# Attention's q and k product from high and low halves, bf16 parts stored once, weights loaded after the rounds

## The reference

```python
x = L0_attn_x                                       # [16, 256, 128] float32
h = _layernorm(x, axis=-1) * (1 + ca) + sa
x = x + ga * _L0_attn_ref(h, L0_attn_w_qkv, ...)
...
qkv = x @ w_qkv + b_qkv                             # inside _L0_attn_ref: 16 heads of depth 8
q = _rope(q)
k = _rope(k)
scores = jnp.einsum('bhtd,bhsd->bhts', q, k) / jnp.sqrt(jnp.float32(D))
attn = jax.nn.softmax(scores, axis=-1)
out = jnp.einsum('bhts,bhsd->bhtd', attn, v)
...
return out @ w_fc + b_fc
```

## Time and profile before

| | us |
|---|---|
| median of 3 runs | 1827.18 (1826.78 to 1829.08) |
| the profiled execution | 1828.58 |
| its span | 1826.5 |
| TensorE busy | 1659.0, 91% |
| VectorE busy | 1366.2, 75% |
| ScalarE busy | 819.6, 45% |
| GpSimd busy | 691.8, 38% |

### The profile page before, as it was taken

How to read it: one execution, slowest core, us unless ns; L and a number is a source line. 1 busy time by engine, 2 the same in 40 slices (tenths; PEclk the granted TensorE clock), 3 DMA queues, 4 the chain that set the end, 5 groups by cost and what they waited for, 6 DMA issues and landing times.

```text
span 1826.5 us, 25499 instructions
## 1 busy us (share of the span) xinstructions
PE 1659.0 (91%) x7212; PEld 1027.0 (56%) x7212; DVE 1366.2 (75%) x2636; ACT 819.6 (45%) x1533; POOL 691.8 (38%) x628
## 2 busy tenths in 40 slices
PE   3888888869989999999999999999998899899999
PEld 2455555446655656556665565655655555555555
DVE  4777777656979988979969889799698587544444
ACT  1566767657644234243352342533525543433333
POOL 2011111100002945928739469187394475000000
PEclk9989989989999999999999999999999999999999
DMA  6554445246575877677767666666671111111110
GB/s 199 152 157 129 119 111 152 89 125 215 180 207 188 222 205 204 210 209 214 215 189 203 187 188 197 189 197 204 190 194 52 41 47 52 35 57 53 52 52 23
DMA packets 172698, 269.49 MB, mean 148 GB/s; under 512 B 23748, under 2 KB 61981, under 8 KB 170053
## 3 DMA queue, kind: packets, MB, share of 16 engines
q1 hardware_dynamic: 168691, 266.33, 49.9%
q10 hardware_dynamic: 1874, 1.36, 0.2%
q0 software_dynamic: 2048, 0.79, 0.2%
HBM read 233.78 MB, written 34.62 MB: 147 GB/s over the span
## 4 chain that ended last, share of the span: by engine, by line
PE 36%; DVE 16%; issue 10%; POOL 10%; ACT 3%; DMA 3%; SPq 1%; DVEq 0%; POOLq 0%; ACTq 0%
PE psum L1528 10%; PE psum L1368 6%; POOL e_prod L1986 6%; PE psum L1370 6%; PE psum L1369 6%; PE psum L1383 5%; DVE psum L1897 4%; POOL e_phi L1986 3%; DVE e_hm L1900 2%; DVE e_vbar L1755 2%; DVE e_y L1755 1%; DVE e_state L1850 1%; DMA e_ring<-w_split 1%; PE psum L1462 1%; DMA rw<-rw_fm 1%
## 5 line engine op out<-in xcount | busy, mean ns | idle before, releaser
L1694 ACT ACTIVATE e_gu<-psum 128x512 f32<-128x512 f32 (+1 forms) x368 | 219.3, 598 | 545.5 <-PE psum L1370 284.3
L1368 PE MATMUL psum<-e_hhi,e_ring 128*128 128x512 f32 x704 | 434.0, 616 | 19.7 <-DMA e_ring<-w_split 11.5
L1383 PE MATMUL psum<-e_hm,w_d 128*128 128x512 f32 (+1 forms) x736 | 382.6, 601 | 15.0 <-DVE e_hm L1903 7.2
L1986 POOL TENSOR_TENSOR e_prod<-e_state,e_phi 128x512 f32<-128x512 f32 x256 | 353.4, 1417 | 2.4 <-POOL e_phi L1986 1.7
L1897 DVE TENSOR_TENSOR psum<-psum,rw 128x512 f32<-128x512 f32 x352 | 243.4, 692 | 90.9 <-PE psum L1370 85.1
L1935 DVE TENSOR_TENSOR e_hm<-psum,rw 128x512 f32<-128x512 f32 x256 | 174.6, 688 | 178.0 <-ACT psum L1722 176.9
L1369 PE MATMUL psum<-e_hhi,e_ring 128*128 128x512 f32 x704 | 279.0, 396 | 0.0
L1370 PE MATMUL psum<-e_hlo,e_ring 128*128 128x512 f32 x704 | 278.8, 396 | 0.0
L1900 DVE TENSOR_TENSOR e_hm<-psum,e_gu 128x512 f32<-128x512 f32 x352 | 243.5, 692 | 39.4 <-ACT e_gu L1694 15.7
L1528 PE MATMUL psum<-e_hm,w_gu 128*128 128x512 f32 x512 | 262.9, 598 | 6.6 <-DVE w_d L1916 5.5
L1722 ACT ACTIVATE psum<-psum 128x512 f32<-128x512 f32 x256 | 148.8, 582 | 254.7 <-PE psum L1370 238.8
(11 more groups left out here) (304 smaller groups left out, 2181.0 us busy)
## 6 DMA issues: line engine op xcount, KB each, us to landing
e_ring<-w_split SPq DMA_DIRECT2D x308, 256.0 KB, 4.2
rw<-rw_fm SPq DMA_DIRECT2D x192, 176.0 KB
qk_parts<-at_part SPq DMA_DIRECT2D x96, 192.0 KB, 3.1
rw<-gates_fm SPq DMA_DIRECT2D x72, 256.0 KB, 3.2
w_split<-e_ring SPq DMA_DIRECT2D x44, 256.0 KB, 2.7
rw<-rw_fm SPq DMA_DIRECT2D x64, 160.0 KB
at_qs<-qk_parts SPq DMA_DIRECT2D x16, 576.0 KB
at_ks<-qk_parts SPq DMA_DIRECT2D x16, 576.0 KB
```

What stands on the lines that cost most here:

```text
L1368: pe.matmul(out, w_hi, x_hi, start=first, stop=False)
L1383: mm = pe.matmul(ps[:, ACC, :], weights_at(T, WD + P * j, P)[0:rows(j), :], hm[0:rows(j), slot(j), :], start=(j == 0), stop=(j == HT - 1))
L1694: a(act_g[0:r, j % 2, :], ps[0:r, GB[j % 2], :], ACT.Silu).then_inc(silu_done, 1)
L1986: ins = tt(out[:, at], x[:, at], y[:, at], op)
```

## The change

The q and k product is made from halves: `w_qk` and each `hb` are rounded to fp32r (`w_hi`, `hb_hi`, ScalarE), the rest after the subtraction is the low half (`w_lo` on VectorE, once; `hb_lo` on GpSimd, each round), and three products, high by high, low by high and high by low, are summed in PSUM. There is one buffer each for `hb_hi` and `hb_lo`. The parts are stored once (two transfers of 192 KB), and each stack is loaded by three transfers of 24 rows; those of `ks` read 8 rows three times. The 16 weight pieces are issued by SP after its last round, when all maxima are in. Buffers of the first gates' work now lie in `rest` and `rest2`. GpSimd's wait for `x_fm` stands in round 2 instead of ahead of the rounds.

```diff
-STACK_DMAS = 2
-OUT_DMAS = 2 * PARTS
+STACK_DMAS = 2 * PARTS
+OUT_DMAS = 2
...
-        bounce = nc.dram_tensor("qk_parts", [BUFS, 2, PARTS, PARTS, DEPTH, HEADS, SEQ], BF16, kind="Internal").ap()
+        bounce = nc.dram_tensor("qk_parts", [BUFS, 2, PARTS, DEPTH, HEADS, SEQ], BF16, kind="Internal").ap()
...
                 if f["proj"]:
-                    pe.wait_ge(h_ready, n + 3)
+                    pe.wait_ge(h_low, n + 3)
...
                     for c in range(2):
-                        mm = pe.matmul(ps[:, M0, c * SEQ:(c + 1) * SEQ], w_qk[:, c * P:(c + 1) * P], hb[:, (k + 2) % BUFS, :],
-                                       start=True, stop=True)
+                        out, at = ps[:, M0, c * SEQ:(c + 1) * SEQ], slice(c * P, (c + 1) * P)
+                        pe.matmul(out, w_hi[:, at], hb_hi[:], start=True, stop=False)
+                        pe.matmul(out, w_lo[:, at], hb_hi[:], start=False, stop=False)
+                        mm = pe.matmul(out, w_hi[:, at], hb_lo[:], start=False, stop=True)
                     mm.then_inc(qk_proj, 1)
...
+            dve.wait_ge(w_high, 1)
+            nc.vector.tensor_tensor(w_lo[:], w_qk[:], w_hi[:].bitcast(F32), ALU.subtract).then_inc(w_cut, 1)
             run(dve, iteration)
...
+                        act.wait_ge(h_ready, n + 4)
+                        if k > FIRST:
+                            act.wait_ge(qk_proj, n + 3)
+                        nc.scalar.activation(hb_hi[:], hb[:, (k + 3) % BUFS, :], ACT.Copy).then_inc(h_high, 1)
...
+            nc.scalar.activation(w_hi[:], w_qk[:], ACT.Copy).then_inc(w_high, 1)
             run(act, iteration)
...
                 if f["p1"]:
                     move_rows(n, k, 0)
+                if f["xn"]:
+                    pool.wait_ge(h_high, n + 4)
+                    nc.gpsimd.tensor_tensor(hb_lo[:], hb[:, (k + 3) % BUFS, :], hb_hi[:].bitcast(F32), ALU.subtract).then_inc(h_low, 1)
                 if f["tail"]:
                     b = n - 2
+                    if k == 2:
+                        pool.wait_ge(T["x_fm_in"], 16)
...
-            pool.wait_ge(T["x_fm_in"], 16)
             run(pool, iteration)
...
             def load_stack(buf, stack, q):
 
-                sp.dma_start(stack[0:ROWS, buf, :, :], bounce[buf, q].rearrange("b a d h t -> (b a d) h t")).then_inc(stacked, 16)
+                for b in range(PARTS):
+                    if q == 0:
+                        src = bounce[buf, 0].rearrange("a d h t -> (a d) h t")
+                    else:
+                        src = bounce[buf, 1, b].unsqueeze(0).broadcast_to([PARTS, DEPTH, HEADS, SEQ])
+                    sp.dma_start(stack[b * PARTS * DEPTH:(b + 1) * PARTS * DEPTH, buf, :, :], src).then_inc(stacked, 16)
...
-                    for i in range(PARTS):
-                        sp.dma_start(bounce[buf, 0, i].rearrange("a d h t -> (d h) a t"), part[:, :, 0:SEQ]).then_inc(part_out, 16)
-                    for i in range(PARTS):
-                        sp.dma_start(bounce[buf, 1, :, i].rearrange("b d h t -> (d h) b t"), part[:, :, SEQ:2 * SEQ])\
+                    for q in range(2):
+                        sp.dma_start(bounce[buf, q].rearrange("a d h t -> (d h) a t"), part[:, :, q * SEQ:(q + 1) * SEQ])\
                             .then_inc(part_out, 16)
-                if k in PIECE_ROUNDS:
-                    for i in range(2):
-                        load_weights(2 * PIECE_ROUNDS.index(k) + i)
 
             run(sp, iteration)
+            for half in range(2):
+                sp.wait_ge(nrows_in[half], 16 * BATCH)
+            for piece in range(WEIGHT_PIECES):
+                load_weights(piece)
+                load_weights(WEIGHT_PIECES + piece)
```

More of the change, by code:

```diff
@@ L45 @@
 FIRST = -3
-STACK_DMAS = 2
-OUT_DMAS = 2 * PARTS
+STACK_DMAS = 2 * PARTS
+OUT_DMAS = 2
 VW = 32
-PIECE_ROUNDS = (0, 1, 2, 3, 13, 14, 15, 16)
 def attention(nc, T, A, x_fm, x_tm, mod):
@@ L72, in attention @@
         hb = sb("at_h", [P, BUFS, SEQ])
+        hb_hi, hb_lo = sb("at_hhi", [P, SEQ], F32R), sb("at_hlo", [P, SEQ], F32R)
+        w_hi, w_lo = sb("at_whi", [P, 2 * D], F32R), sb("at_wlo", [P, 2 * D], F32R)
         qk = sb("at_qk", [P, 2 * SEQ])
@@ L89, in attention @@
         upd = sb("at_upd", [P, SEQ])
-        r0_xc, r0_nt = sb("r0_xc", [P, CHUNK]), sb("r0_nt", [P, CT, D])
-        r0_e, r0_sig, r0_sfc = (sb(f"r0_{n}", [P, CT * EXPERTS]) for n in ("e", "sig", "sfc"))
+        r0_xc, r0_nt = sb("r0_xc", [P, CHUNK]), rest[:].rearrange("p (t d) -> p t d", d=D)
+        r0_e, r0_sig, r0_sfc = rest2[:, 0:CT * EXPERTS], rest2[:, CT * EXPERTS:2 * CT * EXPERTS], sb("r0_sfc", [P, CT * EXPERTS])
         r0_w = r0_e
@@ L117, in attention @@
         h_ready = sem("at_h_ready")
+        w_high = sem("at_w_high")
+        w_cut = sem("at_w_cut")
+        h_high = sem("at_h_high")
+        h_low = sem("at_h_low")
         qk_proj = sem("at_qk_proj")
@@ L313, in iteration @@
                     pe.matmul(ps[:, M1, 0:SEQ], w_fc[:], a_fm[:], start=True, stop=True).then_inc(fc_done, 1)
+            pe.wait_ge(w_cut, 1)
             run(pe, iteration)
@@ L793, in __init__ @@
         self.mean = sem("mean")
-        self.turn = sem("turn")
+        self.turn = T["ln_turn"]
         self.std = sem("std")
@@ L2055, in adaln_two_blocks @@
             T[name] = ctx.enter_context(nc.semaphore(name))
+        T["ln_turn"] = ctx.enter_context(nc.semaphore("ln_turn"))
         T["rb_in"] = [ctx.enter_context(nc.semaphore(f"e_rb_in{s}")) for s in range(RB_SLOTS)]
```

## The result

The change makes the kernel slower: 1854.59 us median (1849.84 to 1858.49) against 1826.98 us for the kernel before beside it (1820.63 to 1829.08); ratio 1.0151, 95% interval 1.0121 to 1.0181. The prediction was 1820, range 1811 to 1850: the sign is wrong and the median lies above the range. The profiled execution took 1849.84 us, span 1847.9, which is 21.4 more than before.

A forecast was written before the change was run, and what follows sets the result against it. Rounds of 18.5 us were taken as bound by TensorE, VectorE and ScalarE handing over work, none filled. Terms -3 + 1 - 2 + 4 - 3 - 5 + 0.5 = -7.5 gave 1821.1, less 1.4: 1820 us, range 1811 to 1850.

The forecast's parts named there:

- start, to the first score product: Before the rounds: halving the weights and first h adds time, fewer part stores save 2 us, loads add 4.2; +4 us.
- rounds 0 and 1, to round 2's first product: Round 1: with no weights queued, TensorE's 4.85 us wait for maxima goes, less what takes its place; -3 us.
- product -3: q and k product: six matmuls of rounded halves replace four passes, 0.2 us less per round; -3 us in 13 rounds.
- low half +1: GpSimd's 0.72 us cut behind both maxima transfers: between nothing and 0.9 us a round, taken as +0.1; +1 us in all.
- waits -2: Inside the rounds: four fewer part stores shorten TensorE's remaining waits on the maxima, 2.55 us at most; taken as -2 us.
- round 15, to the last load of maxima: TensorE's 4.90 us wait goes, as GpSimd's second transfer is issued some 4.4 us earlier; -5 us.
- the loads cost nothing in a round: Three k loads on three engines take 8.7 us but stay hidden, with 1.5 us of slack per 18.5 us round.
- the ring of 17.1 us: Chain from k load issue through first scores to the next k load: 8.4 us plus the load's 8.7 us.
- L: Time from k load issue to the first score product: 1.5 us plus 24 rows at 0.30 us, 8.7 us.
- B: Rival: k load on three engines at 0.5 us a row takes 13.5 us and sets the rounds; 1859 us, chance 0.20.
- D: Rival: k load on three engines at about 0.4 us a row takes 11.1 us; +8, 1828 us, chance 0.13.
- rival E: After the rounds: weights load slowly, at 197 GB/s, and the experts start late; +14, 1833 us, chance 0.10.

## Why the prediction was wrong, step by step

Times of the profiled executions; the sum over the parts is the 22.0 us by which the experts start later (391.64 before, 413.67 after).

| step | predicted | measured |
|---|---|---|
| start, to the first score product | +4 | +3.4 (42.09 to 45.49) |
| rounds 0 and 1, to round 2's first product | -3 | +0.8 (40.81 to 41.61 us) |
| rounds 2 to 13 (product -3, low half +1, waits -2, for 13 rounds) | -4 | +20.6 (237.8 to 258.4 us) |
| round 14 | in the above | +1.8 (17.3 to 19.1) |
| round 15, to the last load of maxima | -5 | -5.6 (28.2 to 22.6 us) |
| end, from that load to the experts | +0.5 | +1.0 (25.5 to 26.5 us) |

**The step that failed is "the loads cost nothing in a round"**, and with it the landing wait that the low half was priced by. I put the k load's cost on its own consumer only, the ring of 17.1 us under a round of 18.5, and asked for none of the other transfers that use the same engines. The landing of the maxima's store I took as free of it: 1.64 to 3.27 us "as now", which gave the low half +0.1 a round and at most 0.9. The runs showed in its place that three pieces of that store come late, with the k rows on their engines: the wait became 4.5 to 5.5 us, and rounds 2 to 13 took 20.6 us longer where -4 was forecast. The bound of 3.27 came from a row of the kernel before, in which no load lies on three engines at that time. It is the load and not the low half's place: stored once without a low half lost 30 us, the halves without the narrow load 7, or nothing in the better place.

**The k load's width and speed were right, and the conclusion wrong.** Three engines (27 packets), 0.31 us a row against 0.30 estimated. The rule of the Trainium skill on the outermost counts, page "DMA: Bandwidth & Descriptors", section "Why a DMA increments its semaphore by 16 and not by 1", holds here: that load's 27 packets are 24 rows and 3 closings. L came out at 9.9 us and not 8.7, from the issue at 247.89 to the last of 72 rows before 257.82 (of the packets from 247.5 to then, 764 less 692 are rows of 8 KB, and none comes later). The 1.5 us ahead of the first row came out (1.51); most rows took 0.31 us, but the three at the start and the three beside the first part stores, which mix in, took 0.7 to 0.9. The ring of 8.4 + L is 18.3: the first scores did not wait for k in the rounds of the loop, as forecast. Only the short round 14, 17.3 us before, fell under the ring, and the first scores at its end waited 1.85 us for k, which is that round's +1.8. "The loads cost nothing in a round" was false in the others too: there they cost through the store of the maxima. Neither B nor D, the rivals with a slow k load, describes it, since both have scores waiting for k in every round. The wait of round 14, and the packets of the load:

```profile
364.60 0.39 PE L196 MATMUL psum<-at_ks,at_qs 72*128 72x256 bf16 x2 [1.85 <-DMA at_ks<-qk_parts]
```

```profile
DMA packets 764, 0.92 MB, mean 89 GB/s; under 512 B 54, under 2 KB 692, under 8 KB 692
...
DMA packets 149, 0.07 MB, mean 53 GB/s; under 512 B 7, under 2 KB 149, under 8 KB 149
```

**A slack that I did not compute.** I read 3.27 us of waiting as a wait of GpSimd; followed on, 219.15 + 2.0 meets the second scores at 221.23, so in that round the chain through the maxima bounded the 18.5 together with TensorE. Then whatever stands behind the landing is not an edge of a range but a price: the halves alone, whose landing is as before, lost 7 us, and lost nothing once the low half lay under the landing.

**The product**: 0.2 us less a round predicted. At full clock a round with the low half out of the way takes 18.34 against 18.5, so 0.16; halves alone, low half between, is 1.0002 of before, so over the whole kernel it does not show.

**Rounds 0 and 1**: the wait of 4.85 went, but where I had allowed for 1.9 us in its place, the product waits 3.67 for the low half (3.45 with the wide k load, so the narrow load is not the reason), and the first score product, at the start, stood 4.08 for k, against 1.88. That the start came out near +4 does not show its terms apart; with the wide k load, and two part stores more, the first score product starts at 43.16, so the narrow load costs some 2.3 us there. Both waits from the timeline:

```profile
45.49 1.04 PE L196 MATMUL psum<-at_ks,at_qs 72*128 72x256 bf16 x4 [4.08 <-DMA at_ks<-qk_parts]
...
62.35 0.58 PE L240 MATMUL psum<-at_hhi,at_whi 128*128 128x256 f32 x1 [3.67 <-POOL at_hlo L558]
```

**Weights behind the rounds**: right. Round 15 gained 5.6, the weights came at the rate of the earlier trace rows, the first gates were stored at 406.28, and the weights behind the rounds alone bring the kernel to 1817.19; rival E fell. The window, the end of GpSimd's queue and SP's store:

```profile
391.00:406.00 15.00, 10.11 (x88) 5.42 (x88) 10.07 (x48) 7.46 (x15) 1.44 (x2) 0.93 1.02 382
```

```profile
387.18 0.56 POOL L544 DMA_DIRECT2D at_qs<-max_parts  x1 [0.32 <-issue]
...
406.28 0.53 SPq L628 DMA_DIRECT2D rw_fm<-r_xc  x1
```

**What was named as a sign of being wrong** was, in the list, a product that waits for at_hlo by more than 0.5 us. It waits 1.9. So the sign was there, without a price.

## What to carry to other kernels

A transfer that uses few DMA engines is not only a long transfer: it takes those engines from every other transfer whose packets are spread over them, and a small transfer is as late as its last packet. The number of its late pieces told here which transfer was in the way: three with three engines taken, eight with eight. Before making a load narrow, list what else is in flight then, and follow the smallest of it to its consumer; if that consumer starts within a few tenths of the landing, the delay is paid in full. A cut of bytes stored (four part stores for six) was worth nothing measurable here, and the narrow load that the further cut to two brought with it cost 32 us; the version with k stored three times and the low half under the landing, and the kernel before with the weights behind the rounds, are each some 9 to 12 us faster than the kernel before. The move of the weights alone is worth as much as the best version of the whole change (1817.19 and 1817.57).

## What the runs showed of the hardware

Eight DMA engines moved 8 KB rows into 8 neighbouring partitions at a time hardly faster than three engines moved them into 24: the whole stack in 7.6 us (77 GB/s, 0.8 us a row) against 8.4 us (70 GB/s, 0.31 us for most rows). The load of 72 rows was through before the store of the maxima went (k stored three times: issued at 230.50, through at 234.89, store at 235.55). In the changed kernel three of the twelve 1 KB pieces of GpSimd's store passed 3.7 to 4.8 us after the issue, while the k load held three engines, and the other nine within 1.6 us. Three issues of a load with a repeated source took 2.18 us of SP's queue, 0.73 each, against 0.31 for the load of 72 rows and 0.33 for one of 8 rows (nine in 2.97).
